# Attention rows beside routed experts: five PE pieces moved to other blocks of a row's order, and a gather's wait split by row

## What is computed

```python
Q, K, V = proj(Wq, bq), proj(Wk, bk), proj(Wv, bv)          # 16 heads of 8, on layernorm(x)
attn = jnp.sin(30.0 * einsum('bhqd,bhkd->bhqk', Q, K) / scale)
x = x + (attn @ V) @ Wo.T + bo
...
xn = layernorm(x)
scores, idx = jax.lax.top_k(sigmoid(xn @ Wr.T + rb), 2)      # 8 experts, 2 for each token
out = shared(xn) + sum over e of cw[..., e] * (silu(xn @ Wg[e].T) * (xn @ Wu[e].T) @ Wd[e].T)
x = x + out
```

## Time and profile before

| | |
|---|---|
| median of 3 runs | 496.52 us (492.93 to 496.62) |
| the profiled execution | 495.03 us, span 493.2 us |
| mean granted TensorE clock | 0.969 |
| busy: PE, ACT, DVE, POOL | 415.2, 335.3, 280.0, 227.4 us |
| first and last sine | 18.5 and 388.5 us |

### The profile page before, as it was taken

The page is one execution under the profiler, slowest core; times in us unless marked ns, Lnnn a source line. Parts: engine busy times, 40 slices in busy tenths (PEclk is TensorE's granted clock), DMA queues, the critical chain, the costliest instruction groups (busy, mean ns, idle before and its releaser), DMA issues.

```text
span 493.2 us, 11542 instructions
## 1 busy us (share of the span) xinstructions
PE 415.2 (84%) x4264; PEld 226.5 (46%) x4264; DVE 280.0 (57%) x890; ACT 335.3 (68%) x428; POOL 227.4 (46%) x269
## 2 busy tenths in 40 slices
PE   2888588978987897989799988898999899859991
PEld 1322123322432243454454445354544598758871
DVE  6787278336453324556536454857555566555884
ACT  1658657967887787778667777677888657644550
POOL 5351162110077213212665576513774778536761
PEclk9999979999999899999999999999999999997996
DMA  5006936943901941189214652697112166831221
GB/s 162 5 1 220 195 98 198 304 97 112 211 26 62 245 87 43 45 233 143 80 50 165 154 116 60 161 198 141 57 60 55 49 122 135 154 96 49 56 66 33
DMA packets 81799, 56.02 MB, mean 114 GB/s; under 512 B 28368, under 2 KB 76112, under 8 KB 81744
## 3 DMA queue, kind: packets, MB, share of 16 engines
q1 hardware_dynamic: 77440, 47.74, 40.5%
q0 software_dynamic: 3584, 7.35, 5.8%
q10 hardware_dynamic: 720, 0.20, 0.2%
HBM read 22.62 MB, written 27.13 MB: 101 GB/s over the span
## 4 chain that ended last, share of the span: by engine, by line
PE 45%; DVE 14%; issue 13%; POOL 8%; ACT 8%; SPq 6%; DMA 6%; ACTq 0%; DVEq 0%; POOLq 0%
PE o_ps L670 13%; PE score L657 7%; POOL hid_lo L1486 3%; PE tile_ps L788 3%; ACT attn L920 3%; DVE hid L1256 3%; PE tile_ps L790 3%; PE tile_ps L789 3%; ACT gate L941 2%; DVE x_all L1301 2%; SPq L513 2%; POOL y_back L1508 2%; PE r_ps L683 2%; DMA y_back<-in_wd 2%; PE tile_ps L810 2%
## 5 line engine op out<-in xcount | busy, mean ns | idle before, releaser
L920 ACT ACTIVATE attn<-score 128x1024 f32<-128x1024 f32 x256 | 247.6, 1025 | 59.0 <-PE score L657 58.7
L1486 POOL TENSOR_TENSOR hid_lo<-hid,hid_hi 128x512 f16<-128x512 f32 (+1 forms) x55 | 62.3, 1132 | 158.2 <-DVE hid_hi L1263 143.8
L670 PE MATMUL o_ps<-attn,vals 128*32 128x512 f32 x1024 | 127.6, 617 | 0.0
L657 PE MATMUL score<-queries,keys 64*128 64x512 f16 x512 | 82.6, 388 | 16.1 <-ACT attn L920 8.9
L1256 DVE SCALAR_TENSOR_TENSOR hid<-tile_ps,gate 128x512 f32<-128x512 f32 (+1 forms) x52 | 35.0, 674 | 60.9 <-ACT gate L941 60.8
L657 PEld LDWEIGHTS score<-queries,keys 64*128 64x128 f16 x512 | 19.1, 94 | 93.7 <-ACT attn L920 59.4
L670 PEld LDWEIGHTS o_ps<-attn,vals 128*32 128x32 f32 x1024 | 27.2, 111 | 64.3 <-issue 62.3
L941 ACT ACTIVATE gate<-tile_ps 128x512 f32<-128x512 f32 (+1 forms) x52 | 30.4, 584 | 30.8 <-PE tile_ps L790 30.7
L788 PE MATMUL tile_ps<-xt,w_hi 128*128 128x128 f16 x244 | 43.1, 220 | 6.9 <-DVE y_sb L1277 3.4
L790 PE MATMUL tile_ps<-xt,w_lo 128*128 128x128 f16 x244 | 43.1, 219 | 0.0
L789 PE MATMUL tile_ps<-xt,w_hi 128*128 128x128 f16 x244 | 43.1, 219 | 0.0
(11 more groups left out here) (222 smaller groups left out, 954.0 us busy)
## 6 DMA issues: line engine op xcount, KB each, us to landing
y_sorted<-y_sb SPq DMA_DIRECT2D x40, 128.0 KB
q_four<-q_parts SPq DMA_DIRECT2D x14, 256.0 KB
k_four<-k_minus SPq DMA_DIRECT2D x14, 256.0 KB
queries<-q_four SPq DMA_DIRECT2D x14, 256.0 KB
keys<-k_four SPq DMA_DIRECT2D x14, 256.0 KB
x_sorted<-zeros SPq DMA_DIRECT2D x2, 1472.0 KB, 11.9
queries<-q_three SPq DMA_DIRECT2D x14, 192.0 KB
keys<-k_three SPq DMA_DIRECT2D x14, 192.0 KB
```

Of the source, the lines that this page charges most:

```text
L657: mm = pe.matmul(score[h][:, i, :], keys[b % 2][rows, 2 * j + h, kt * P:(kt + 1) * P], queries[b % 2][rows, 2 * j + h, :], start=True, sto ...
L670: mm = pe.matmul(o_ps[32 * i:32 * i + 32, :], vals[b % 2][:, kt, h:h + 32], attn[k % RING][:, i, :], start=(k == 0), stop=(k == UNITS - 1))
L920: act.activation(attn[k % RING][:, 2 * (u % 2):2 * (u % 2) + 2, :], score[u % 2][:, :, :], ACT.Sin, scale=SIN_SCALE).then_inc(sined, 1)
L1486: pool.tensor_tensor(hid_lo[d % HB][:, :, cols(d)], hid[d % HR][:, :, cols(d)], hid_hi[d % HB][:, :, cols(d)], ALU.subtract).then_inc(lo_b ...
```

## The change

Nothing is computed otherwise. Three things change:
- the slot tables. On PE the first turn goes from step 2 to 0, Q from 6 to 4, V from 10 to 8, the second turn from 14 to 12, the ranks from 22 to 20: all from duo blocks to values blocks, behind the sums. K (6), `project_out` (2) and `route` (14) stay in duo blocks. The copies, the second norm, the splits, the stores and loads and the scatters move by one to three slots with them. `load_queries` and `store_k` now have the same slot number, and `load_queries` stands first in the code.
- `copy_o` and `copy_xt` are both at slot 1, right behind the second sine of a row, and `copy_o` stands ahead of `copy_xt`; in the tail `copy_o` goes from slot 1 to 0.
- a gather of group 1 or 2 waits, at the first gather of each row, for the combination of the same row of the group before; until now the first gather of a group waited for both rows. And `y_sb` has four buffers in place of three (YR).

The planner gives the same duos at the same slots. Gathers of group 1 move from slots 245, 246, 248, 262 to 280 to 245, 246, 260 to 279; those of groups 2 and 3 stay at 287 to 309 and 311 to 321.

```diff
-S_XT1, S_OUT, S_Q, S_K, S_V, S_XT2, S_ROUTE, S_PREFIX = 2, 2, 6, 6, 10, 14, 14, 22
-S_COPYO, S_COPYX1, S_SCALEQ, S_SCALEK, S_COPYX2 = 2, 3, 7, 8, 15
-S_QHI, S_QLO, S_KHI, S_KLO, S_PLACEV, S_KNEG = 8, 9, 10, 11, 12, 13
-S_STOREQ, S_LOADQ, S_STOREK, S_LOADK = 10, 14, 13, 19
+S_XT1, S_OUT, S_Q, S_K, S_V, S_XT2, S_ROUTE, S_PREFIX = 0, 2, 4, 6, 8, 12, 14, 20
+S_COPYO, S_COPYX1, S_SCALEQ, S_SCALEK, S_COPYX2 = 1, 1, 5, 8, 13
+S_QHI, S_QLO, S_KHI, S_PLACEV, S_KLO, S_KNEG = 6, 7, 9, 10, 11, 12
+S_STOREQ, S_LOADQ, S_STOREK, S_LOADK = 8, 12, 12, 18
...
-S_DISPATCH, S_SCATTER = 23, 26
...
+S_DISPATCH, S_SCATTER = 21, 24
...
-XT, GR, HR, HB, YR = 3, 2, 2, 4, 3
+XT, GR, HR, HB, YR = 3, 2, 2, 4, 4
...
+                if 1 <= b < ROWS and s == S_COPYO and b not in DVE_COPIES:
+                    copy_o(b - 1)
+                if tail == E_COPYO:
+                    copy_o(ROWS - 1)
...
                 if (row, t, c) == (0, 0, 0):
                     for i in range(YR):
                         pool.wait_ge(y_stored[i], 16 * len(range(i, LAST_RANK[g] + 1, YR)))
-                    if 0 < g < len(ROUTE_GROUPS) - 1:
-                        pool.wait_ge(combined, combined_rows(g - 1, len(ROUTE_GROUPS[g - 1]) - 1))
+                if (t, c) == (0, 0) and 0 < g < len(ROUTE_GROUPS) - 1:
+                    pool.wait_ge(combined, combined_rows(g - 1, row))
```

More of the change, by code:

```diff
@@ L64 @@
 TAIL = ROWS * SLOTS
-S_XT1, S_OUT, S_Q, S_K, S_V, S_XT2, S_ROUTE, S_PREFIX = 2, 2, 6, 6, 10, 14, 14, 22
-S_COPYO, S_COPYX1, S_SCALEQ, S_SCALEK, S_COPYX2 = 2, 3, 7, 8, 15
-S_QHI, S_QLO, S_KHI, S_KLO, S_PLACEV, S_KNEG = 8, 9, 10, 11, 12, 13
-S_STOREQ, S_LOADQ, S_STOREK, S_LOADK = 10, 14, 13, 19
+S_XT1, S_OUT, S_Q, S_K, S_V, S_XT2, S_ROUTE, S_PREFIX = 0, 2, 4, 6, 8, 12, 14, 20
+S_COPYO, S_COPYX1, S_SCALEQ, S_SCALEK, S_COPYX2 = 1, 1, 5, 8, 13
+S_QHI, S_QLO, S_KHI, S_PLACEV, S_KLO, S_KNEG = 6, 7, 9, 10, 11, 12
+S_STOREQ, S_LOADQ, S_STOREK, S_LOADK = 8, 12, 12, 18
 S_STATS1, S_AGGR1, S_POW1, S_APPLY1, S_ADDBO = 27, 28, 28, 29, 31
-S_RES, S_STATS2, S_AGGR2, S_POW2, S_APPLY2, S_XHI, S_XLO = 5, 6, 6, 7, 8, 10, 11
+S_RES, S_STATS2, S_AGGR2, S_POW2, S_APPLY2, S_XHI, S_XLO = 4, 5, 5, 6, 7, 9, 10
 S_LOGIT, S_TANH, S_TOP, S_CHOOSE = 16, 17, 18, 19
-S_DISPATCH, S_SCATTER = 23, 26
-E_COPYO, E_OUT, E_RES, E_POW2, E_APPLY2, E_XHI, E_XLO = 1, 2, 3, 4, 5, 7, 8
+S_DISPATCH, S_SCATTER = 21, 24
+E_COPYO, E_OUT, E_RES, E_POW2, E_APPLY2, E_XHI, E_XLO = 0, 2, 3, 4, 5, 7, 8
 E_XT2, E_COPYX2, E_ROUTE, E_LOGIT, E_TANH, E_TOP, E_CHOOSE = 10, 10, 12, 12, 12, 13, 14
@@ L997, in _ @@
                 if 1 <= b < ROWS:
-                    if s == S_COPYO and b not in DVE_COPIES:
-                        copy_o(b - 1)
                     if s == S_COPYX2 and b not in DVE_COPIES:
@@ L1003, in _ @@
                         tanh_half(b - 1)
-                if tail == E_COPYO:
-                    copy_o(ROWS - 1)
                 if tail == E_COPYX2:
@@ L1394, in _ @@
                 if b in DVE_COPIES:
+                    if b and s == S_COPYO:
+                        copy_o(b - 1)
                     if ahead == S_COPYX1:
@@ L1400, in _ @@
                         scale_k(b + 1)
-                    if b and s == S_COPYO:
-                        copy_o(b - 1)
                     if b and s == S_COPYX2:
```

## The result

The changed kernel took **489.58 us** (median of 4, 488.63 to 491.95) beside 496.57 of the kernel before: a ratio of 0.988, 95% interval 0.9835 to 0.9925. The profiled execution took 490.00, its span is 488.2. A second pair, in a later group of runs, took 488.08 and 494.68 when profiled, with medians of 489.22 and 495.6: 0.9882 (0.9845 to 0.9919). So it is 7 us or 1.2% faster, where 16 were forecast.

The account below looks back on a forecast made before the run. No single engine bounds the kernel: PE has 45% of the chain, is full in rows 4 to 7, neither engine full in rows 1 and 2. Terms sum to 16.1 off 495.0, giving 478.9; forecast 480 us, range 474 to 488.

Parts of the forecast that it names:

- The tail, 8.0 and 1.2: Tail: PE's 5.17 us wait for hid_lo and 2.8 of half clock go (8.0); project_out loses its 1.18 wait (1.2).
- Row 3, 3.8: Row 3: 2.2 of 5.8 us of waits come back, plus 1.6 of clock; 3.8 us gained (2.2 to 4.5).
- The clock term, 1.6: Row 3, from slot 16: the clock no longer falls, as the layout's longest idle is about 1; 1.6 us gained.
- Rows 1 and 2, 0.5: Rows 1 and 2: blocks behind the sums grow by 3.2 us against regained waits; 0.5 gained (-2 to +2).
- Row 2's keys, 1.4: Start of row 2: keys come 3 to 5 us earlier and PE's 1.89 wait goes; 1.4 us gained.
- Row 1's keys, 0 (-2.4 to +2.8): Before row 1: key loads issued later; 0 if DMA engines limit, row up to 2.4 us later or 2.8 earlier.
- Rows 4 to 7, 1.2: Rows 4 to 7: 1.7 us of PE idle goes, a y_sb wait may grow by up to 0.9; 1.2 gained (0 to 2).
- the front gives nothing: Rival: pieces behind the sums cost in full, regained waits only pay for it; 485 to 486 us, chance 0.17.
- The slower rival: Rival: blocks behind the sums starve ScalarE in three or four rows without full PE; 498 to 500 us, chance 0.04.

Follow-up runs that it names:

- v_ranks: Changed kernel with V at slot 10 and place_v at 12 in rows 0 to 2, ranks, dispatch and scatters at 22, 23, 26: 479.63 us (median of 6), ratio 0.9683.
- tail_only_2: Kernel before with only the gather wait split by row, second run: 489.01 us, ratio 0.9892.
- v_back: Changed kernel with V at slot 10 (from 8) and place_v at 12 (from 10) in rows 0 to 2: 482.93 us, single run.
- 495 profiles: Profiles of runs in the faster of two run conditions, where the kernel before took 495.6 us; in the other it took 521 to 524.
- before_v8: Kernel before with V at slot 8 (from 10) and place_v at 10 (from 12) in rows 0 to 2: ratio 1.0096, in the slower 521 us conditions.
- scale_k7: Changed kernel with scale_k at slot 7 (from 8) in rows 0 to 2: slots 8 to 12 of row 1 took 6.25 us in place of 6.76.
- store_first: Changed kernel with the query loads at slot 13 (from 12), so key stores go out first: 488.42 us, single run.
- v_all: Changed kernel with V at slot 10 and place_v at 12 in every row: 484.03 us (median of 4), ratio 0.976.
- yr3: Changed kernel with three y_sb buffers in place of four: 489.49 us.

## Why the prediction was wrong, point by point

**The tail, 8.0 and 1.2.** The gate did what its steps said. From the last `down` ahead of the idle time (the 19th of the tail's 38, at 436.26 before and 439.04 after) to the end of the span it is 57.0 against 49.2: 7.8 for a forecast 8.0, idle and half clock together. `project_out` did lose its 1.18. But 12 us later the wait for a `hid_lo` was 2.46 (0.77 before). I had priced the gate and `project_out`, and not what the ranks' new place does to the gathers here. With the ranks back (`v_ranks`) that wait is 0.88, and the part up to the 19th `down` takes 45.4 us, 1.0 less than in `tail_only_2`: the forecast 1.2, nearly whole.

**Row 3, 3.8.** The layout held: slots 0 to 16 took 24.6 and take 22.7, 1.9 for 2.2. The clock term, 1.6, failed: slots 16 to 20 went from 6.30 to 6.55. "The longest idle in my layout is about 1, so I take it" was the wrong step. In `v_back` the term came (5.09), though nothing in row 3 differs: PE's waits of 0.91, 0.53, 0.58, 0.36 and 0.53 ahead of the sums are the same in both. It came in all three 495 profiles with V at 10 in rows 0 to 2, and in none of the four with V at 8 there (6.5 to 6.7); so what decides seems to lie ahead of row 3, and what it is stays open. The prediction set the Trainium skill's rule (TensorE: Matmul & The Clock Gate, Why this matters for your kernels), that a pause brings the half clock back, against it and left the term open by the rule. Here the same short pauses were followed by either clock, so my reading of the longest idle doesn't tell when, and neither does the rule.

**Rows 1 and 2, 0.5.** This step failed most. Working per piece, I let four blocks grow by 3.2 and set waits of "about 1 before each" against it. The waits did go. What I missed is in two runs: with V alone behind the sums a row pays V's full 1.1 (`before_v8`), and in the changed kernel K is done early but VectorE scales it late, so V also waits for `scale_k`, 1.20 in row 1, 0.5 of which the earlier scaling took away (`scale_k7`). The two are 2.3 of the 2.5 that slots 8 to 12 of row 1 grew by. I had called the order Q, K, V free of waits since "K waits for nothing", and did not lay out VectorE, which does the weight splits at that time.

**Row 2's keys, 1.4.** Wrong in sign. I took the slots in the table for the time of the work: V a block and `k_neg` a slot earlier, so keys 3 to 5 us earlier. In fact `place_v` went ahead of the low key half on a full VectorE, which reached it 2.0 later, counted from row 1's first sine, and the key stores behind query loads on SyncE. Undoing either did not bring the keys back: counted from row 1's first sine they were issued after 30.8 before (31.3 in `tail_only_2`), 32.1 and 31.4 in the two profiles of the changed kernel, 31.5 in `v_back` and 31.7 in `store_first`. So neither order alone is the cause, and what holds them stays open.

**Row 1's keys, 0 (-2.4 to +2.8).** -1.1 and -1.3, inside, but by luck as much as by reading, since unchanged code differs by 1.5 there. The Trainium skill (DMA: Bandwidth & Descriptors, Queues, rings and completion order) has each DMA engine take the descriptors of one ring in ring order; the prediction drew from it that the keys would be late by their issue, which they were not. The issue was late by 5.6 and the keys by 1.1, an issue 5.8 earlier won about 0.6, and in `v_all` keys issued at 52.16 were there at 60.26, earlier than those issued at 48.53 before (61.36). So most of an earlier issue is lost here; that the DMA engines are the limit (their share is 1.10 from 57.0 to 62.5) fits, but was not tested by itself.

**Rows 4 to 7, 1.2.** 1.9 and 1.6, but by two large terms that I did not have, so the number is near by luck: row 5 gained 2.5 and 2.3, and the ranks took 1.3, 2.1 and 0.6 in slots 20 to 24 of rows 4, 6 and 7. Both are the ranks' (most of row 5's gain is the clock behind the shorter wait for `y_sb`). I had priced V's effect on another wait for `y_sb`, had said that the wait at slot 30 keeps its place, where it went from 2.33 to 1.37, and never costed the ranks, the last of the five moved pieces; the step to lay out was VectorE's list, where places come ahead of the bank's copy.

**In sum.** The forecast missed by 9.6. The steps that failed most are V's place in rows 0 to 2, taken as "even", and the ranks, taken at nothing. With both put back the kernel takes 479.63, 9.9 less than `yr3` in the same group; 1.4 of it is the clock in row 3, so the match with the forecast 480 is not to be trusted to the microsecond.

**The rivals.** Closest was "the front gives nothing", but the front gave less than nothing. The slower rival's mechanism, blocks behind sums that cost in full, is the one that acted, at 1.1 for V in the early rows, and only there, as it had said (for the other pieces it was not tested); but I priced it as all or nothing.

What stays open: what sets the clock in row 3, what delays row 2's keys, and what the turn, Q, the second turn and the copies give one by one.

## What to carry to other kernels

A gate that asks for more than its own data is worth looking for first: two lines made all of the gain, and five moved pieces together gave none. But a sum of nothing can hide large terms: with two of the five put back (V in the early rows, the ranks) the rest took 9.4 us off the gate alone. Try such pieces one by one. Where two engines alternate and neither is full, a piece in the block that feeds the other engine can cost its full length (V did), so move pieces only where a wait is longer than that. And when a piece moves on one engine, write out the list of the engine that copies its result: half of V's cost in row 1 and the ranks' loss in row 6 sat in VectorE's order (the scaling of K, the places ahead of the bank's copy), not on PE.
